# A graph kernel: chunk sums aligned to a chunk's own first target, and one-hot rings eight units deep

## The reference

```python
dst = (12500 * uniform(400000) ** 2).astype(int32)      # sorted; low targets have far more edges
def L0(x, src, dst, attr, g, mu, sigma, root_w, bias):
    gauss = exp(sum(-0.5 * (attr[:, None] - mu) ** 2 / (1e-14 + sigma ** 2), -1))   # [E, 3]
    msg = einsum('eko,ek->eo', (x[src] @ g).reshape(E, 3, 64), gauss)
    aggr = segment_sum(msg, dst) / maximum(segment_sum(1, dst), 1)
    return silu(aggr + x @ root_w + bias + x)
def sage(h, W_self, W_neigh, b):
    return h @ W_self + segment_sum(h[src], dst) / maximum(deg, 1) @ W_neigh + b
x = layernorm(x + L0(x, ...))
x = layernorm(x + sage(relu(sage(x, ...1)), ...2))
```

## Time and profile before

| | us |
|---|---|
| median of 3 runs | 8203.81 (8200.99 to 8227.09) |
| profiled execution | 8277.25 |
| its span in the trace | 8275.3 |
| the 98 tiles, in the trace | 364 to 6780 |
| two large products and all behind them | 6880 to 8275 |

### The profile page before, as it was taken

How to read it: one execution, slowest core, us unless ns; L and a number is a source line. 1 busy time by engine, 2 the same in 40 slices (tenths; PEclk the granted TensorE clock), 3 DMA queues, 4 the chain that set the end, 5 groups by cost and what they waited for, 6 DMA issues and landing times.

```text
span 8275.3 us, 120249 instructions
## 1 busy us (share of the span) xinstructions
PE 4795.9 (58%) x21035; PEld 3512.1 (42%) x21036; DVE 5058.5 (61%) x14764; ACT 3721.3 (45%) x8949; POOL 3273.6 (40%) x3173
## 2 busy tenths in 40 slices
PE   1455555555545555445545555444444446999999
PEld 1123333333333433233333334333333335877777
DVE  4566566656555555556555656544454447888888
ACT  2212344444434343333433434344444434888887
POOL 3013455545554455445555545555555410000000
PEclk5557777777777777677767777777777767999999
DMA  2001111121111111112111111121211132777777
GB/s 66 26 15 30 46 44 43 42 49 42 42 42 41 46 44 42 29 40 50 42 46 45 42 49 42 41 50 42 50 42 41 41 62 80 254 251 244 247 249 224
DMA packets 498147, 612.98 MB, mean 74 GB/s; under 512 B 135126, under 2 KB 347652, under 8 KB 496916
## 3 DMA queue, kind: packets, MB, share of 16 engines
q1 hardware_dynamic: 392228, 495.60, 19.1%
q0 software_dynamic: 101568, 106.16, 7.3%
q10 hardware_dynamic: 4054, 8.11, 0.5%
HBM read 437.03 MB, written 172.56 MB: 74 GB/s over the span
## 4 chain that ended last, share of the span: by engine, by line
PE 23%; DVE 20%; issue 19%; another core or an unknown queue 13%; DVEq 12%; ACT 7%; DMA 4%; ACTq 1%; SPq 0%; POOLq 0%; POOL 0%
PE pw L904 8%; DVE rE L1412 4%; PE pw L1080 4%; PE pw L929 4%; DMA rA<-count 3%; ACT rE L611 3%; PE pw L1086 3%; DVEq L1622 3%; DVE rE L1472 2%; DVEq L1445 2%; ACT rB L650 2%; DVE rE L1410 2%; PE pw L876 2%; DVE rE L1540 1%
## 5 line engine op out<-in xcount | busy, mean ns | idle before, releaser
L548 POOL DMA_INDIRECT rE<-in_x,idx x3136 | 3238.4, 1033 | 3430.5 <-issue 3426.5
L650 ACT CAST rB<-pw 128x792 uint8<-128x792 f32 x1568 | 1258.7, 814 | 3797.6 <-remote 1104.1
L904 PE MATMUL pw<-rE 128*128 128x193 f32 x7824 | 1900.6, 411 | 1056.4 <-DVE rE L1472 911.6
L904 PEld LDWEIGHTS pw<-rE 128*128 128x128 f32 x7824 | 1749.4, 248 | 1281.8 <-DVE rE L1472 1046.8
L929 PE MATMUL pw<-rE 128*128 128x396 f16 x3840 | 869.0, 377 | 939.9 <-DVE rE L1412 374.2
L611 ACT ACTIVATE rE<-rE,cols 128x64 f32<-128x64 f32 x4704 | 1257.9, 344 | 31.8 <-issue 23.0
L1412 DVE TENSOR_SCALAR rE<-iperm,gr 128x392 f16<-128x392 f16 x3840 | 1075.8, 320 | 93.6 <-issue 90.8
L754 ACT ACTIVATE aring<-rA,scl 128x1024 fp32r<-128x1024 uint8 (+2 forms) x800 | 1026.2, 1327 | 217.7 <-DMA rA<-count 200.1
L1843 DVE TENSOR_SCALAR dring<-rA,scl 128x2048 fp32r<-128x2048 uint8 (+2 forms) x800 | 914.5, 1177 | 160.3 <-DMA rA<-count 142.2
L929 PEld LDWEIGHTS pw<-rE 128*128 128x128 f16 x3840 | 385.9, 107 | 1348.8 <-issue 676.9
L923 PE MATMUL pw<-rE 128*128 128x396 f16 x1600 | 394.1, 368 | 770.4 <-ACT rB L650 352.6
(11 more groups left out here) (271 smaller groups left out, 3088.9 us busy)
## 6 DMA issues: line engine op xcount, KB each, us to landing
rA<-count SPq DMA_DIRECT2D x672, 384.0 KB, 3.9
count<-rB SPq DMA_DIRECT2D x98, 1344.0 KB
rE<-in_x,idx POOLq DMA_INDIRECT x3136
rA<-count SPq DMA_DIRECT2D x96, 448.0 KB, 4.2
count<-rB SPq DMA_DIRECT2D x110, 224.0 KB, 2.2
cols<-cols_d SPq DMA_DIRECT2D x98, 64.0 KB
rA<-count SPq DMA_DIRECT2D x28, 192.0 KB, 2.5
cols_d<-rA SPq DMA_DIRECT2D x3, 1568.0 KB, 5.2
```

The lines of the kernel that those rows point to most:

```text
L548: pool.indirect_dma_start(out=gath[:, s, u * CB + b, :], out_offset=None, in_=x, in_offset=bass.IndirectOffsetOnAxis(ap=idx[:, s, u * CB + ...
L650: act.copy(stage[:, s, :, j * 2 * W:(j + 1) * 2 * W].rearrange("p h (w n) -> p w h n", w=2), pu[j % 3][:, :, 0:CW].rearrange("p w (h n) -> ...
L904: ins = pe.matmul(sums[side][:, 0:AW], onehot[:, side, bb, :], wgath[:, side, bb, :], start=(bb == 0), stop=(bb == CB - 1))
```

## The change

1. **One pass for a chunk.** A chunk's one-hots begin at its least target (`first` is now a node, not a group), so that 128 nodes from there take in all its targets if the targets span fewer than 128. The table's `many` is now the span of the targets over 128, plus 1. `onehot` is built from a window of `iota_x` (0..127 twice) rotated by `back`, so that node `i` of a group has its sum in row `i` whichever group it is in.
2. **Two masked additions.** The 128 sums belong to group `tile` from row `row` on and to `tile + 1` below it. `add_sums` now adds twice, each time with a column of 0s and 1s (`from_row`, `below_row`).
3. **Rings of eight units** (`RU = 8`). `comp` moves to the free half of `rB`. The waits for `a_used` follow.
4. **A later list.** The list and `base_of` stand after unit 3 (merged, one pair) or 1 (two pairs). Before it PE waits until unit 2 is copied out; unit 5 (or 2) waits for `x_add`.
5. POOL's clearing of a part of `rB` (line 556) now waits for `s_bound`, behind the last tile.

```diff
-RU = 4
+RU = 8
+LATE = 4
...
-        comp = rE[:, o:o + RU * 4 * CW // 2].bitcast(F16).rearrange("p (r b c) -> p r b c", r=2 * RU, b=2)
-        o_lo = o + RU * 4 * CW // 2
+        comp = rB[:, HP * P // 2:HP * P // 2 + RU * 4 * CW // 2].bitcast(F16).rearrange("p (r b c) -> p r b c", r=2 * RU, b=2)
+        o_lo = o
...
+            pool.wait_ge(s_bound, 1)
             pool.memset(rB[:, 2 * HP * P // 4:3 * HP * P // 4], 0.0).then_inc(f_clr, 1)
...
                     for n in range(u * NU // U, (u + 1) * NU // U):
-                        if late and n == 2:
+                        at = LATE // max(1, pairs_w) - 1
+                        if late and n == (at + 3) // 3 * 3 - 1:
 
                             pe.wait_ge(x_add, pe.snap(xk, min_val=1, max_val=1 << 24))
                             pe.sem_inc(s_tick[0], 1)
                         unit(t, n, pairs_w)
-                        if late and n == 2 // max(1, pairs_w) - 1:
+                        if late and n == at:
+                            if at > 2:
+                                pe.wait_ge(a_evac, t * NU + 5)
+                                pe.sem_inc(s_tick[0], 1)
 
                             listed(other)
...
+            V.tensor_scalar(from_row[:], iota[:], pidx[:, 0:1], None, ALU.is_le)
+            V.tensor_scalar(below_row[:], iota[:], pidx[:, 0:1], None, ALU.is_gt)
...
-            link(V.tensor_copy(ci[0:NT], cf[0:NT]))
-            link(V.tensor_scalar(ci[0:NT], ci[0:NT], 7, None, ALU.logical_shift_right))
-            link(V.tensor_copy(cf[0:NT], ci[0:NT]))
             link(V.tensor_tensor(cf[0:NT, 1, :], cf[0:NT, 1, :], cf[0:NT, 0, :], ALU.subtract))
+            link(V.tensor_copy(ci[0:NT, 1, :], cf[0:NT, 1, :]))
+            link(V.tensor_scalar(ci[0:NT, 1, :], ci[0:NT, 1, :], 7, None, ALU.logical_shift_right))
+            link(V.tensor_copy(cf[0:NT, 1, :], ci[0:NT, 1, :]))
...
                 dve.wait_ge(a_comb[side], done)
-                dve.wait_ge(a_add, k)
-                V.tensor_tensor(a, sums[side][:, 0:AW], a, ALU.add).then_inc(a_add, 1)
+                dve.sem_inc(s_tick[3], 1)
+                dve.wait_ge(a_add, k * 2 - 1)
+                dve.sem_inc(s_tick[3], 1)
+                for at, mask in ((t, from_row), (after, below_row)):
+                    a = acc[:, bass.ds(at, 1), :].rearrange("p t a -> p (t a)")
+                    if mask is below_row:
+                        dve.wait_ge(a_add, k * 2)
+                        dve.sem_inc(s_tick[3], 1)
+                    V.scalar_tensor_tensor(a, sums[side][:, 0:AW], mask[:, bass.ds(r, 1)], a, ALU.mult, ALU.add).then_inc(a_add, 1)
...
+                    node = nc.s_assert_within(dve.snap(c * P + first), 0, NT * P - 1,
+                                              skip_runtime_bounds_check_because="the last of many begins at a node of the chunk or below")
+                    tile = dve.snap(node // P, min_val=0, max_val=NT - 1)
+                    row = dve.snap(node % P, min_val=0, max_val=P - 1)
+                    back = dve.snap(P - row, min_val=1, max_val=P)
...
-                    V.tensor_scalar(local[:], here[:, 0, :], tile128[:, bass.ds(tile, 1)], None, ALU.subtract).then_inc(a_loc, 1)
+                    V.tensor_scalar(local[:], here[:, 0, :], tile128[:, bass.ds(tile, 1)], iota[:, bass.ds(row, 1)],
+                                    ALU.subtract, ALU.subtract).then_inc(a_loc, 1)
                     add_sums(k, side)
                     dve.wait_ge(a_loc, k)
-                    V.tensor_tensor(onehot[:, side], iota[:, None, :].broadcast_to([P, CB, P]),
+                    dve.sem_inc(s_tick[3], 1)
+                    V.tensor_tensor(onehot[:, side], iota_x[:, bass.ds(back, P)][:, None, :].broadcast_to([P, CB, P]),
...
-                        free = n + 1 if behind < 2 else max(n + 1, min(n + 3, 4))
+                        free = n + 1 if behind < 2 else max(n + 1, min(RU // 2 + 1 + n // 2, RU))
...
-                        if n == 1:
+                        if n == LATE - 1:
 
                             listed(q - 1, other)
                             base_of(q, t)
...
-                        if late and n == 2 // pairs_w - 1:
+                        if late and n == LATE // pairs_w - 1:
```

More of the change, by code:

```diff
@@ L39 @@
 PK = 4096
+PN = 16384
 DT = 2
@@ L1348, in _ @@
             V.tensor_scalar(win_p[:], iota[:, 0:JW], float(GW * P), None, ALU.mult)
-            V.memset(comp[:].rearrange("p r b c -> p (r b) c")[:, :, GW:CW], 0.0)
             V.memset(scl[:, 0:2], 1.0)
@@ L1373, in _ @@
             prev = [dve.alloc_register(f"prev{k}") for k in range(2)]
+            turn = [dve.alloc_register(f"turn{k}") for k in range(2)]
             xr = dve.alloc_register("xr")
@@ L1381, in _ @@
                 dve.reg_mov(prev[k], 0)
+                dve.reg_mov(turn[k], 0)
                 dve.reg_mov(cs[k], 1)
@@ L1475, in prepare @@
                     dve.reg_mov(prev[side], tile)
+                    dve.reg_mov(turn[side], row)
                     dve.reg_add(cs[side], cs[side], 1)
```

25 lines of the change are left out of this document (15 added, 10 removed).

## The result

The changed kernel takes 8675.56 us (median of 4 runs, 8662.90 to 8693.29), the kernel before 8202.40 in the same comparison (8198.47 to 8227.09): ratio 1.057, with a 95% interval of 1.054 to 1.060. The forecast was 7800 us, so faster. The profiled execution of the changed kernel takes 8664.3 us, near its median.

The account below looks back on a forecast made before the run. Bound by waits between PE and DVE in the three loops, no engine full. Second passes −388, second addition +118, rings and list −141 sum to −411: 7866 us profiled, 7793 as a median, forecast 7800, range 7450 to 8100.

Parts of the forecast that it names:

- second passes go: Chunk sums in the loops: 97 second passes vanish, 4.0 us each, −388 us (ends −97 and −1100).
- second addition: DVE's chunk sums: 392 more masked additions at 0.40 us, 0.3 after hiding, +118 us (ends 0 and +314).
- rings of eight: Three loops, 94 tiles: DVE runs further ahead, fewer slot waits; −141 us together with the later list (ends −639 and +188).
- later list: Three loops: DVE's 6.57 us wait should shrink and PE's idle move; inside the −141 us, +188 if only adding waits.
- A part is hidden: DVE's second addition: idle in each tile hides some of its 0.40 us, leaving 0.3 each, 392 times.
- a wait moves more often than it goes ... I take −1.5: Rings and list, three loops: PE and DVE feed each other, so only 1.5 us a tile is gained over 94 tiles.
- Rival (c): Merged and one-pair tiles: later list delays the next tile 3.6 us, 81 tiles, +292; about 8560 us in all; chance 0.05.
- the loads reach two tiles ahead, and idle at 1455 is small: Loads of columns and indices: the argument against the later list delaying the next tile, a case given chance 0.05.
- The sign I had named for it: PE's idle ahead of the second chunk's pass: above 6 us would show the later list delaying tiles.
- Rival (b): POOL's gathers set the tile's period, many loop C tiles at 59 to 60 us; 8090, up to 8180 us; chance 0.2.
- Rival (d): Loops' matmuls: PE's granted clock falls to 0.70 from 0.74, 157 us more if none is hidden, 7960 us; chance 0.05.
- its mark of 0.71: PE in the loops: a granted clock below 0.71 would show that PE's clock falls.

Follow-up runs that it names:

- p1_oneadd: p12_fit without the second masked addition and its register steps; 7865.52 us, ratio 0.954.
- p12_fit: a_fit with rings of four units and the list and waits where they stood before, so one pass and two additions alone; 8085.49 us, ratio 0.985.
- a_list1: a_fit with the list back at its old place, rings still eight units deep; 8035.39 us, ratio 0.976.
- a_fit: a_tick0 with 26 counter increments put once ahead of loop B, so its code lies in an estimated 3 blocks; 8311.86 us, ratio 1.013.
- a_tick0: The changed kernel without three of its four new counter increments in a chunk's turn; 8672.02 us, ratio 1.057.
- p345_fit: The kernel before with only the rings of eight, later list and POOL's clearing changed, loop B's code in an estimated 3 blocks; 8459.59 us, ratio 1.028.
- b_w: The kernel before with POOL waiting after each chunk's eight gathers until they have landed; 7337.55 us, ratio 0.894.
- d_list1: a_list1 with each chunk's eight gathers replaced by one plain transfer of 1024 rows; 6526.35 us, ratio 0.814.
- b_pad40: The kernel before with 40 counter increments on DVE put once ahead of loop B; 8338.91 us, ratio 1.013.
- w_tick0: w_fit without the 26 counter increments ahead of loop B, so its code lies in an estimated 4 blocks again; 7475.75 us, ratio 0.911.
- d_fit: a_fit with each chunk's eight gathers replaced by one plain transfer of 1024 rows; 6813.45 us, ratio 0.850.
- w_fit: a_fit with POOL waiting after each chunk's eight gathers, not the last chunk's alone, until they have landed; 7265.48 us, ratio 0.906.

## Why the prediction was wrong, step by step

| term | predicted | measured | from |
|---|---|---|---|
| second passes go | −388 | −361 | p1_oneadd against before |
| second addition | +118 | +232 | p12_fit against p1_oneadd |
| rings of eight | −141 together with the list | −62 | a_list1 against p12_fit |
| later list | (in the −141) | +289 | a_fit against a_list1 |
| loop B's code in 4 blocks | none | +360 | a_tick0 against a_fit |
| sum | −411 | +458 | a_tick0 is +457, the changed kernel +473 |

Each measured term is the step from one kernel to the next, the kernel before subtracted, so the sum comes out by itself. That two terms can be added is shown only for the halves (p345_fit).

**Second passes.** Right in kind and size, 3.7 us each for 4.0, with the dearer masked addition (0.42 us for 0.36) already inside. The size is in part luck: no row chose the middle between the 1.0 of whole tiles and the 7.1 of the last tile, and by loop it is 4.8, 4.0 and 3.2 us a pass in A, B and C where I had read 6, 2 and 6.

**Second addition.** The mechanism was right, the size half. Each takes 0.42 us (line 1416) where I had bounded it by the plain addition's 0.36, and between the two DVE is idle for 0.44 (173.0 us over 394 in p12_fit; 0.68 in the changed kernel) where it was 0.03 between the chained steps in the earlier trace rows: there one step follows another by a counter alone, here register steps of 0.26 and 0.05 us stand between them. "A part is hidden" failed in the tiles of two pairs, where with four units the delay came back as 8.7 us a tile of waiting for a free slot.

**Rings and list.** The step that failed is "a wait moves more often than it goes ... I take −1.5". I had put two things into one term, with ends −639 and +188. The ring was worth −62. I had read all of the 6.8 us a tile at 1539 as a wait for a slot; the earlier trace rows puts 86.0 of the 156 us down to "issue", and that is DVE's register load (line 1445), which no ring takes away. At most 2.9 us a tile were the ring's, and in the changed kernel that wait is gone (0.3) while the line's idle is still 5.2. That a wait moves was right. The list was worth +289, outside my ends. Rival (c) had the place and the mechanism. That its size fits too, 3.6 us in each of 81 tiles, +292, is luck: it is 0.5 us a tile in loop B, 5.5 in C and 2.8 in A. Its chance of 0.05 rested on "the loads reach two tiles ahead, and idle at 1455 is small", which speaks of the loads; the cost is DVE's wait for PE's product at the old line 1604, 3.19 us in the earlier trace rows, which I had read and not followed: PE gets two units and a pass more ahead of the list, so that wait is where to look for growth. The sign I had named for it, idle ahead of the second chunk's pass, isn't where it shows.

**Code.** The step is missing, and it is the largest miss. A loop's body grew from 346 to 383 instructions, and I costed the added register steps by their time alone. The page of the kernel before had a row for it that I left out: "q14 instruction" moves 215 packets in the kernel before, 157 of them in loop A, whose body holds six tiles, and 8 in loop B. With that and the two lengths the question would have been there. Without this term the measured ones make +98 (a_fit: +97, ratio 1.013), and the change would still have been slower.

**Rival (b)** was wrong as put (no period of 59 us holds; tiles of loop C went to 55.3), but the runs of gathers cost more than any term of my sum (10.6% of the kernel before, b_w), and the change doesn't touch them. **Rival (d)** is there as a follower: granted clock 0.68 and 0.67 in loops B and C for 0.72 and 0.74, below its mark of 0.71, and a pass 4.4 us of PE (1731.1 over 392) for 3.9. How much of these 0.5 us is on the path isn't shown. PE is idler in both loops than before (busy 49 and 42% of the time for 51 and 49%), and where the waits went (d_list1, PE busy 61 and 59%) the clock is 0.79 in both. That PE's idle time lowers the clock would fit these numbers and has no run of its own.

## What to carry to other kernels

Before an edit adds instructions to a loop's body, count the body and look at the "instruction" queues by loop: here loop B's 371 instructions ran with 162 packets in 32 turns (a_tick0) and, with 26 idle instructions ahead of them, with 8 (a_fit), 360 us faster. The price was 3.4 (b_pad40), 4.6 (w_tick0) and 11.4 us a turn (a_tick0). When a handshake is moved behind other work, price what is now ahead of it on the engine that answers, and look for the cost where the asker waits. Where many gathers are issued in a row, look at the other engines' small steps in the later part of the run; a pause after every eight was worth 10.6% here, one after every sixteen nothing. When an idle time is put down to "issue", look into the engine's queue before you take it for a wait that the change will shorten: 3.7 us a tile were a register load here.

## What the hardware showed that I hadn't expected

A long run of indirect gathers goes with a slow instruction stream on DVE from between the 8th and the 16th gather on (in a_fit 7.4 instructions in a us at the first gather, 0.6 to 1.2 from the eleventh to the fifteenth). Late in a run of 24 ACT's single steps come 1.4 us apart, and PE stood 14.84 us waiting for ACT. With plain transfers of the same bytes none of it is seen, and the kernels are 16% (d_fit on a_fit) and 17% (d_list1 on a_list1) faster. What in the chip does it wasn't found. The kernel before took 8006 and 8027 us on two chips and 8202 to 8227 us in the comparisons on others: a spread of 2.8%, where its runs on one chip lie within 1.3%. That is why each ratio here is taken against the kernel before on its own chip. The pause kernels w_fit and w_tick0, on two chips whose kernels before differ by 2.6%, agree within 0.6% in merged tiles, so a ratio doesn't carry from one chip to another for every kernel.
